# Local attention: the token shift ahead of the feed-forward made by three transfers within SBUF in place of TensorE products with shift matrices

## The chip, the cores and the metric

The kernel runs on one core of a Trainium2 chip. A core has five engines that run their own instruction lists and meet only at semaphores: TensorE (PE in the profile; PEld is its weight load), VectorE (DVE), ScalarE (ACT), GpSimd (POOL) and SyncE (SP), which here only issues transfers. The metric is the device time of one execution in microseconds (us), lower is better.

## The reference

A four-stage model over 8 sequences of 256 tokens of 128 features: dense attention, a routed feed-forward of 16 experts, a similarity counter, and last two layers of local attention with a gated feed-forward. Only the last stage is touched. Cut to what matters:

```python
def shift_token(t):
    t1, t2 = jnp.split(t, 2, axis=-1)                      # two halves of the features
    t2 = jnp.pad(t2, ((0, 0), (1, 0), (0, 0)))[:, :-1]     # second half: from the token before
    return jnp.concatenate([t1, t2], axis=-1)

def _layer(x, wqkv, qs, ksc, wo, lg, lb, w1, b1, w2, b2):
    h = shift_token(x)
    q, k, v = jnp.split(h @ wqkv, 3, axis=-1)              # to 8 heads of 64
    ...                                                    # l2norm, rotary, windows of 64 tokens
    x = x + o @ wo
    h = shift_token(x)                                     # the shift of this change
    h = (h - h.mean(-1, keepdims=True)) / jnp.sqrt(h.var(-1, keepdims=True) + 1e-05) * lg + lb
    a, g = jnp.split(h @ w1 + b1, 2, axis=-1)
    return x + (a * gelu(g)) @ w2 + b2
for l in range(2):
    x = _layer(x, ...)
```

## The kernel before

All arithmetic is f32 (the mask is bf16). The last stage works on 16 units, a unit being one layer of one sequence: 256 tokens as two tiles of 128 partitions (TB = 2), each with 128 features. Unit m is layer m // 8 of sequence m % 8. The stage is a software pipeline written out by hand: `run_steps` calls `step(n)` on each engine for n = -3 to 17, and the order of the calls inside an engine's `step` is the order of its instructions. In step n the attention of unit n runs beside the feed-forward of unit n - 1, the projections of units n + 1 and n + 2, and the end of unit n - 2. Nothing is scheduled by a planner; an engine that waits holds up all that stands behind it in its own list.

The names of one unit, with the lines of the kernel before:

- `scores1(n, a)`, PE: the mask (L1437) and the scores (L1450) of head pair a = 0 to 3. It waits for `f_e`, the exponentials of the pair before, since both use PSUM banks 0 and 1.
- `neg_max` on DVE (L1966, L1968) and `expo` on ACT (L1020, four exponentials each with its sum) follow every `scores1`.
- `attn_out(m)`, PE (L1484): the output projection; `residual_mid(m)`, DVE (L1989), adds the residual into SBUF tile `xm` and raises `f_xm`.
- `shift_mid(m)`, PE (L1492 to L1494): three f32 products of `xm` with the identity, with a shift matrix and with a carry matrix (for the first row of the second tile) leave the shifted tokens in the right half of PSUM bank 6 and raise `f_sh`.
- `stats_mid(m)`, DVE: `ln_stats` (L1566, L1569, L1571) on the shifted tokens; `ln_rstd`, POOL (L791): the power -1/2; `normed_mid(m)`, DVE: `ln_apply` (L1575).
- `turn_normed` (L1500), `hidden` (L1513) and `ffn_out` (L1523) on PE, `gelus` (L1047) on ACT, `gate` (L2013) on DVE: the feed-forward.
- `project1` (L1392), PE, and `rotate`, DVE (L1940 to L1949): queries and keys of unit n + 2, one quarter i after the other through one PSUM bank, with `square` on ACT (L994) between. `project_v` (L1406), PE: values of unit n + 1. `turn_probs1` (L1461) and DVE's `probs_out` (L1985): the turned probabilities.
- POOL: `add_rot` (L771), `normalise1` (L795), `copy_x` (L762), `inverse_norm` (L780, a power).

In SP's list the last stage has only the five stores of the result (L570): each waits for `h_out`.

Of the kernel before, what the change touches and what calls it, by code (L numbers as in the profile page):

```python
# [7 lines left out]
ALU = mybir.AluOpType  # L8
# [3 lines left out]
P = 128  # L12
# [43 lines left out]
def build_program(nc, A, out):  # L56

    with ExitStack() as ctx:
# [13 lines left out]
        identb = sb("identb", [P, P], BF16)  # L72
        causal = sb("causal", [P, P])
        band = sb("band", [P, TB, P], BF16)
        shift = sb("shift", [P, P])
        batch_rows = sb("batch_rows", [P, B])
        carry = sb("carry", [P, P])
        mhalf = sb("mhalf", [P, TB * H1])
        onecol = sb("onecol", [P, 1])
        lower = sb("lower", [P, P])  # L80
# [296 lines left out]
        rs1 = two(from_scratch, 2, TB)  # L377
        oT1 = two(from_scratch, PAIRS1, S)
        xm = two(from_scratch, TB, D)
        hn = from_scratch(TB, D)  # L380
        h2T = from_scratch(S)
        gl = from_scratch(3, S)
# [72 lines left out]
        def _(sp_):  # L455
# [109 lines left out]

            outc = out.rearrange("b (t p) d -> p (b t) d", p=P)
            for e, (o, n) in enumerate(ENDS):
                sp_.wait_ge(h_out, e + 1)
                sp_.dma_start(outc[:, o:o + n, :], x5[:, o:o + n, :]).then_inc(out_sem, 16)  # L570
            sp_.wait_ge(out_sem, 16 * len(ENDS))

        @block.gpsimd
        def _(pool):
            def row_rstd(c):
# [10 lines left out]
            pool.affine_select(out=causal[:], in_=causal[:], compare_op=ALU.is_ge, fill=0.0, base=0,  # L587
                               pattern=[[-1, P]], channel_multiplier=1)
            pool.memset(band[:], 0.0)
            pool.memset(shift[:], 0.0)  # L590
            pool.memset(carry[:], 0.0)
            pool.memset(batch_rows[:], 1.0)
            pool.memset(lower[:], 1.0)
            pool.memset(ones[:], 1.0)
# [4 lines left out]
                               pattern=[[0, TB], [-1, P]], channel_multiplier=1)  # L599
            pool.affine_select(out=batch_rows[:], in_=batch_rows[:], compare_op=ALU.is_ge, fill=0.0, base=0,  # L600
                               pattern=[[-H0, B]], channel_multiplier=1)
            pool.affine_select(out=shift[:], in_=shift[:], compare_op=ALU.not_equal, fill=1.0, base=1,
                               pattern=[[-1, P]], channel_multiplier=1)
            pool.drain()
            row_rstd(1)
            pool.affine_select(out=band[:], in_=band[:], compare_op=ALU.is_ge, fill=NEG, base=WIN,
                               pattern=[[0, TB], [1, P]], channel_multiplier=-1)
            pool.affine_select(out=batch_rows[:], in_=batch_rows[:], compare_op=ALU.is_ge, fill=0.0, base=H0 - 1,
                               pattern=[[H0, B]], channel_multiplier=-1)
            pool.affine_select(out=carry[:], in_=carry[:], compare_op=ALU.not_equal, fill=1.0,  # L610
                               base=-(P - 1), pattern=[[-1, P]], channel_multiplier=1)
            pool.drain()
            row_rstd(2)
            pool.memset(band[0:WIN, 1, WIN:P], 0.0)
# [464 lines left out]
        def _(pe):  # L1079
# [405 lines left out]
                                       start=(a == 0), stop=(a == PAIRS1 - 1))  # L1485
                mm.then_inc(f_wo, 1)

            def shift_mid(m, s):

                pe.wait_ge(f_xm, m + 1)  # L1490
                o = bank(6)[:, S:2 * S].rearrange("p (t d) -> p t d", t=TB)
                pe.matmul(o[:, :, 0:64], ident[:], xm[s][:, :, 0:64], start=True, stop=True, skip_group_check=True)  # L1492
                pe.matmul(o[:, :, 64:P], shift[:], xm[s][:, :, 64:P], start=True, stop=False, skip_group_check=True)
                pe.matmul(o[:, 1, 64:P], carry[:], xm[s][:, 0, 64:P], start=False, stop=True,  # L1494
                          skip_group_check=True).then_inc(f_sh, 1)

            def turn_normed(m):
                pe.wait_ge(f_hn, m + 1)
                for t in range(TB):
# [27 lines left out]
            def step(n, s):  # L1527
                if live(n + 2): project1(n + 2, s, 0)
                if live(n): scores1(n, s, 1)
                if live(n): turn_qk(n, s, 3)  # L1530
                if live(n - 1): attn_out(n - 1, 1 - s)
                if live(n): turn_probs1(n, 0)
                if live(n): scores1(n, s, 2)
                if live(n - 1): shift_mid(n - 1, 1 - s)
                if live(n + 1): project_v(n + 1, 1 - s, 0)
                if live(n + 1): project_v(n + 1, 1 - s, 1)
                if live(n): turn_probs1(n, 1)
                if live(n): values1(n, s, 0)
                if live(n): scores1(n, s, 3)
                if live(n + 2): project1(n + 2, s, 1)  # L1540
                if live(n + 1): turn_qk(n + 1, 1 - s, 0)
                if live(n - 1): turn_normed(n - 1)
                if live(n - 2): ffn_out(n - 2)
                if live(n + 3): turn_x(n + 3)
                if live(n): values1(n, s, 1)
                if live(n): turn_probs1(n, 2)
                if live(n + 2): project1(n + 2, s, 2)
                if live(n + 1): turn_qk(n + 1, 1 - s, 1)
                if live(n - 1): hidden(n - 1, 1)
                if live(n + 1): scores1(n + 1, 1 - s, 0)  # L1550
                if live(n): turn_probs1(n, 3)
                if live(n + 2): project1(n + 2, s, 3)
                if live(n): values1(n, s, 2)
                if live(n - 1): hidden(n - 1, 0)
                if live(n): values1(n, s, 3)
                if live(n + 1): turn_qk(n + 1, 1 - s, 2)
# [5 lines left out]
        def _(dve):  # L1562
# [364 lines left out]
                dve.memset(hT[s][64:P, 0:1], 0.0)  # L1927
            dve.memset(ssx[:], 1e-24)
            dve.memset(hg[64:P, 2, :], 1.0)
            dve.drain().then_inc(const_ready, 1)  # L1930
            dve.sem_inc(f_x, B)

# [62 lines left out]
                                  bank(7)[:, 0:S].rearrange("p (t d) -> p t d", t=TB), ALU.add).then_inc(f_x, 1)  # L1995

            def stats_mid(m):
                dve.wait_ge(f_sh, m + 1)
                ln_stats(lambda t: bank(6)[:, S + t * P:S + (t + 1) * P], TB, 0, f_var)

            def normed_mid(m):
                dve.wait_ge(f_rstd, m + 1)
                ln_apply(lambda t: hn[:, t, :], lambda t: bank(6)[:, S + t * P:S + (t + 1) * P],
                         TB, 0).then_inc(f_hn, 1)

            def gate(m):
                dve.wait_ge(f_a, m + 1)
# [108 lines left out]
```

## Time and profile before

| | |
|---|---|
| median of 3 runs | 933.12 us (931.44 to 933.57) |
| span of the profiled execution | 933.2 us |
| last stage, units 0 to 15 | from about 490 us to the end |
| busy over the span | PE 85%, DVE 71%, ACT 63%, POOL 57% |
| granted TensorE clock, mean | 0.927 of full speed |

The page gives the profiled execution's time as its span alone, 933.2 us, 0.1 us from the median. In the middle of the last stage one unit follows the other at a constant distance, so one unit can be read for all; the last four units run with less work beside them and are read one by one.

### The profile page before, as it was taken

The page shows a single profiled execution, that of the slowest core. Times are in us where ns is not written, and L with a number is a line of the kernel's source. Part 1 is how long each engine was busy: PE and PEld are TensorE (multiplying, and loading weights), DVE is VectorE, ACT ScalarE, POOL GpSimd, SP SyncE. Part 2 cuts the span into 40 slices and gives each one's busy share as a digit, 9 for nine tenths or more (in the row PEclk, how much of TensorE's full clock was granted, in tenths as well). Part 3 has the DMA queues.
Part 4 walks back from the last instruction along what each step waited for, and adds up shares of the span by engine and source line. Part 5 has one row for each costly group of instructions (what it writes and reads, how often), then busy time and mean ns, then how long its engine had stood idle before and what let it go on. Part 6 is the DMA issues. An engine that isn't in the chain of part 4 may idle for free. (4 is left out here: it accounts for less than half of the span.)

```text
span 933.2 us, 21526 instructions
## 1 busy us (share of the span) xinstructions
PE 789.5 (85%) x6366; PEld 587.0 (63%) x6366; DVE 663.4 (71%) x1986; ACT 588.5 (63%) x1784; POOL 527.3 (57%) x603
## 2 busy tenths in 40 slices
PE   5999999999989735982664789999999999998884
PEld 4777777777769735871551356666666666666664
DVE  5777777777776755553675577888888888887555
ACT  3688888888850103761441468888888888886660
POOL 4644444444442773326834867777777777775411
PEclk9999999999999856995785799999999999999998
DMA  8544444444400292431100000000000000000001
GB/s 223 186 156 152 152 152 152 152 152 152 152 27 1 61 311 64 113 96 46 43 12 0 1 1 2 1 2 2 1 2 1 1 2 2 1 2 2 12 2 34
DMA packets 61823, 61.28 MB, mean 66 GB/s; under 512 B 13244, under 2 KB 50607, under 8 KB 61615
## 3 DMA queue, kind: packets, MB, share of 16 engines
q1 hardware_dynamic: 59694, 56.10, 18.1%
q0 software_dynamic: 2048, 4.20, 1.6%
q8 instruction: 39, 0.64, 0.3%
q14 instruction: 42, 0.34, 0.1%
HBM read 17.55 MB, written 23.00 MB: 43 GB/s over the span
## 5 line engine op out<-in xcount | busy, mean ns | idle before, releaser
L643 POOL TENSOR_TENSOR scratch<-scratch 128x256 f32<-128x256 f32 (+1 forms) x128 | 105.7, 826 | 129.9 <-DVE scratch L1621 128.4
L1020 ACT ACTIVATE scratch<-psum,scratch 128x128 f32<-128x128 f32 x256 | 113.8, 458 | 49.2 <-DVE scratch L1968 47.4
L771 POOL TENSOR_TENSOR big<-big 128x512 f32<-128x512 f32 x64 | 81.2, 1269 | 70.1 <-DVE big L1949 70.1
L875 ACT ACTIVATE scratch<-psum,scratch 128x256 f32<-128x256 f32 x256 | 117.7, 478 | 2.9 <-DVE scratch L1639 2.8
L780 POOL TENSOR_TENSOR scratch<-scratch,mhalf 128x16 f32<-128x16 f32 x32 | 93.0, 2905 | 16.3 <-DVE scratch L1955 16.3
L1940 DVE TENSOR_REDUCE scratch<-big 128x8 f32<-128x512 f32 x64 | 43.7, 683 | 45.5 <-ACT big L994 45.3
L1125 PE MATMUL psum<-scratch 128*128 128x256 f32 x240 | 61.7, 380 | 0.0
L1632 DVE TENSOR_TENSOR psum<-psum,causal 128x512 f32<-128x512 f32 x64 | 44.8, 700 | 22.9 <-PE psum L1148 22.8
L1148 PE MATMUL psum<-scratch 64*128 64x128 f32 (+1 forms) x512 | 59.3, 350 | 0.0
L1169 PE MATMUL psum<-scratch 128*64 128x256 f32 (+1 forms) x512 | 55.7, 339 | 1.6 <-ACT scratch L884 1.6
L994 ACT ACTIVATE big<-psum 128x512 f32<-128x512 f32 x64 | 38.5, 602 | 29.0 <-PE psum L1392 28.9
L1158 PE MATMUL psum<-ident,scratch 128*128 128x128 f32 x384 | 56.0, 282 | 0.6 <-POOL scratch L643 0.5
L865 ACT ACTIVATE scratch<-psum,scratch 128x256 f32<-128x256 f32 x60 | 28.4, 474 | 42.9 <-PE psum L1125 42.9
L1966 DVE TENSOR_REDUCE scratch<-psum 128x4 f32<-128x512 f32 x64 | 44.0, 687 | 15.2 <-PE psum L1450 14.0
L875 ACT ACTIVATION_READ_ACCUMULATOR scratch<-psum,scratch 128x1 f32 x256 | 54.0, 211 | 0.0
L1020 ACT ACTIVATION_READ_ACCUMULATOR scratch<-psum,scratch 128x1 f32 x256 | 52.3, 204 | 0.0
L1169 PEld LDWEIGHTS psum<-scratch 128*64 128x64 f32 x512 | 31.1, 136 | 31.7 <-issue 20.2
L1472 PEld LDWEIGHTS psum<-scratch,big 128*64 128x64 f32 x768 | 34.5, 138 | 22.0 <-issue 21.5
L1158 PEld LDWEIGHTS psum<-ident,scratch 128*128 128x128 f32 x384 | 40.8, 140 | 11.9 <-issue 10.5
L795 POOL TENSOR_TENSOR scratch<-scratch 128x512 f32<-128x512 f32 x32 | 33.2, 1038 | 23.1 <-DVE scratch L1977 23.1
L1947 DVE TENSOR_TENSOR big<-psum,rot 128x512 f32<-128x512 f32 x64 | 43.5, 680 | 1.8 <-POOL big L771 1.8
L1437 PE MATMUL psum<-band,identb 128*128 128x256 bf16 x128 | 24.8, 276 | 23.2 <-ACT scratch L1020 21.7
(288 smaller groups left out, 2272.0 us busy)
## 6 DMA issues: line engine op xcount, KB each, us to landing
routed_in<-zfill SPq DMA_DIRECT2D x64, 256.0 KB, 2.1
scratch<-w_qkv SPq DMA_DIRECT2D x60, 193.0 KB, 2.2
scratch<-xT SPq DMA_DIRECT2D x60, 128.0 KB, 2.1
scratch<-routed_in SPq DMA_DIRECT2D x47, 64.0 KB, 1.9
routed_out<-scratch SPq DMA_DIRECT2D x23, 128.0 KB, 1.9
big<-in_L_ffn_W SPq DMA_DIRECT2D x1, 2048.0 KB, 8.7
stream<-in_L_attn_resid_pre SPq DMA_DIRECT2D x4, 256.0 KB, 3.6
big<-in_L_ffn_b SPq DMA_DIRECT2D x1, 1024.0 KB, 11.9
```

Source lines behind the costliest of these rows:

```text
L643: pool.tensor_tensor(y, y, rs[s][:, t, :].unsqueeze(2).to_broadcast([P, 2, n]), ALU.mult).then_inc(b_p, 1)
L771: pool.tensor_tensor(qk[s][t][:, j * INNER:(j + 1) * INNER], t1[i % 2], t2[i % 2], ALU.add).then_inc(f_add, 1)
L780: pool.tensor_tensor(o, ss[:, :, j * H1:(j + 1) * H1], half, ALU.pow).then_inc((f_rq, f_rk)[j], 1)
L875: last = act.activation(pr[s][:, t, h, :], scores_of(s)[:, h, t * S:(t + 1) * S], ACT.Exp, bias=nb[s][:, 2 * t + h:2 * t + h + 1], accum_o ...
L1020: last = act.activation(p1[k][:, h, t, :], bank(h)[:, t * P:(t + 1) * P], ACT.Exp, bias=nb1[k][:, h, t:t + 1], scale=rq8[s][:, t, 2 * a + ...
L1125: mm = pe.matmul(bank(6)[:, j * S:(j + 1) * S], w[:, j * P:(j + 1) * P], x, start=True, stop=True)
L1148: mm = pe.matmul(scores_of(s)[:, h, t * S:t * S + (t + 1) * P], qT[s][h * DH:(h + 1) * DH, t * P:(t + 1) * P], kT[s][h * DH:(h + 1) * DH, ...
L1158: mm = pe.transpose(turned_bank(h)[:, (kt + t) * P:(kt + t + 1) * P], pr[s][:, t, h, kt * P:(kt + 1) * P], ident[:])
L1169: mm = pe.matmul(bank(7)[h * 64:(h + 1) * 64, S + kt * P:2 * S], vS[r][:, kt, h * 64:(h + 1) * 64], pt[h][:, kt * S:kt * S + (TB - kt) * P ...
L1632: dve.tensor_tensor(diagonal, diagonal, mask, ALU.mult)
L1940: dve.tensor_reduce(ssx[:, t, j * H1:(j + 1) * H1, 0], o3(sq1[i % 2]), AX.X, ALU.add)
L1966: dve.tensor_reduce(mx1[k][:], psum[:, 0:2, 0:S].rearrange("p h (t n) -> p h t n", t=TB), AX.X, ALU.max)
```

## The change

`shift_mid` leaves PE's list and becomes three transfers in SP's list, from `xm` to a new SBUF tile `hs`: the second feature half one partition down, the row that crosses from the first tile to the second, and the first feature half unmoved. All three raise `f_sh`, and DVE's statistics wait for the three together. `ln_stats` and `ln_apply` read `hs` in place of PSUM bank 6. `hs` exists once; its one row without a token before it is set to zero once. The two matrices are no longer made on POOL. The five stores of the result stand between the transfers of the last units.

```diff
@@ -72,9 +72,7 @@
         identb = sb("identb", [P, P], BF16)
         causal = sb("causal", [P, P])
         band = sb("band", [P, TB, P], BF16)
-        shift = sb("shift", [P, P])
         batch_rows = sb("batch_rows", [P, B])
-        carry = sb("carry", [P, P])
         mhalf = sb("mhalf", [P, TB * H1])
         onecol = sb("onecol", [P, 1])
         lower = sb("lower", [P, P])
@@ -377,6 +375,7 @@
         rs1 = two(from_scratch, 2, TB)
         oT1 = two(from_scratch, PAIRS1, S)
         xm = two(from_scratch, TB, D)
+        hs = from_scratch(TB, D)
         hn = from_scratch(TB, D)
         h2T = from_scratch(S)
         gl = from_scratch(3, S)
@@ -565,9 +564,26 @@
 
 
             outc = out.rearrange("b (t p) d -> p (b t) d", p=P)
-            for e, (o, n) in enumerate(ENDS):
+
+            def shift_mid(m):
+
+                y = xm[m % 2]
+                sp_.wait_ge(f_xm, m + 1)
+                sp_.dma_start(hs[1:P, :, DH:D], y[0:P - 1, :, DH:D]).then_inc(f_sh, 16)
+                sp_.dma_start(hs[0:1, 1, DH:D], y[P - 1:P, 0, DH:D]).then_inc(f_sh, 16)
+                sp_.dma_start(hs[:, :, 0:DH], y[:, :, 0:DH]).then_inc(f_sh, 16)
+
+            def put_out(e):
+                o, n = ENDS[e]
                 sp_.wait_ge(h_out, e + 1)
                 sp_.dma_start(outc[:, o:o + n, :], x5[:, o:o + n, :]).then_inc(out_sem, 16)
+
+            for m in range(UNITS):
+                shift_mid(m)
+                if m in (UNITS - 4, UNITS - 2):
+                    put_out((m - UNITS + 4) // 2)
+            for e in range(2, len(ENDS)):
+                put_out(e)
             sp_.wait_ge(out_sem, 16 * len(ENDS))
 
 
@@ -587,8 +603,6 @@
             pool.affine_select(out=causal[:], in_=causal[:], compare_op=ALU.is_ge, fill=0.0, base=0,
                                pattern=[[-1, P]], channel_multiplier=1)
             pool.memset(band[:], 0.0)
-            pool.memset(shift[:], 0.0)
-            pool.memset(carry[:], 0.0)
             pool.memset(batch_rows[:], 1.0)
             pool.memset(lower[:], 1.0)
             pool.memset(ones[:], 1.0)
@@ -599,16 +613,12 @@
                                pattern=[[0, TB], [-1, P]], channel_multiplier=1)
             pool.affine_select(out=batch_rows[:], in_=batch_rows[:], compare_op=ALU.is_ge, fill=0.0, base=0,
                                pattern=[[-H0, B]], channel_multiplier=1)
-            pool.affine_select(out=shift[:], in_=shift[:], compare_op=ALU.not_equal, fill=1.0, base=1,
-                               pattern=[[-1, P]], channel_multiplier=1)
             pool.drain()
             row_rstd(1)
             pool.affine_select(out=band[:], in_=band[:], compare_op=ALU.is_ge, fill=NEG, base=WIN,
                                pattern=[[0, TB], [1, P]], channel_multiplier=-1)
             pool.affine_select(out=batch_rows[:], in_=batch_rows[:], compare_op=ALU.is_ge, fill=0.0, base=H0 - 1,
                                pattern=[[H0, B]], channel_multiplier=-1)
-            pool.affine_select(out=carry[:], in_=carry[:], compare_op=ALU.not_equal, fill=1.0,
-                               base=-(P - 1), pattern=[[-1, P]], channel_multiplier=1)
             pool.drain()
             row_rstd(2)
             pool.memset(band[0:WIN, 1, WIN:P], 0.0)
@@ -1485,15 +1495,6 @@
                                        start=(a == 0), stop=(a == PAIRS1 - 1))
                 mm.then_inc(f_wo, 1)
 
-            def shift_mid(m, s):
-
-                pe.wait_ge(f_xm, m + 1)
-                o = bank(6)[:, S:2 * S].rearrange("p (t d) -> p t d", t=TB)
-                pe.matmul(o[:, :, 0:64], ident[:], xm[s][:, :, 0:64], start=True, stop=True, skip_group_check=True)
-                pe.matmul(o[:, :, 64:P], shift[:], xm[s][:, :, 64:P], start=True, stop=False, skip_group_check=True)
-                pe.matmul(o[:, 1, 64:P], carry[:], xm[s][:, 0, 64:P], start=False, stop=True,
-                          skip_group_check=True).then_inc(f_sh, 1)
-
             def turn_normed(m):
                 pe.wait_ge(f_hn, m + 1)
                 for t in range(TB):
@@ -1531,7 +1532,6 @@
                 if live(n - 1): attn_out(n - 1, 1 - s)
                 if live(n): turn_probs1(n, 0)
                 if live(n): scores1(n, s, 2)
-                if live(n - 1): shift_mid(n - 1, 1 - s)
                 if live(n + 1): project_v(n + 1, 1 - s, 0)
                 if live(n + 1): project_v(n + 1, 1 - s, 1)
                 if live(n): turn_probs1(n, 1)
@@ -1927,6 +1927,7 @@
                 dve.memset(hT[s][64:P, 0:1], 0.0)
             dve.memset(ssx[:], 1e-24)
             dve.memset(hg[64:P, 2, :], 1.0)
+            dve.memset(hs[0:1, 0, DH:D], 0.0)
             dve.drain().then_inc(const_ready, 1)
             dve.sem_inc(f_x, B)
 
@@ -1995,13 +1996,12 @@
                                   bank(7)[:, 0:S].rearrange("p (t d) -> p t d", t=TB), ALU.add).then_inc(f_x, 1)
 
             def stats_mid(m):
-                dve.wait_ge(f_sh, m + 1)
-                ln_stats(lambda t: bank(6)[:, S + t * P:S + (t + 1) * P], TB, 0, f_var)
+                dve.wait_ge(f_sh, (m + 1) * 3 * 16)
+                ln_stats(lambda t: hs[:, t, :], TB, 0, f_var)
 
             def normed_mid(m):
                 dve.wait_ge(f_rstd, m + 1)
-                ln_apply(lambda t: hn[:, t, :], lambda t: bank(6)[:, S + t * P:S + (t + 1) * P],
-                         TB, 0).then_inc(f_hn, 1)
+                ln_apply(lambda t: hn[:, t, :], lambda t: hs[:, t, :], TB, 0).then_inc(f_hn, 1)
 
             def gate(m):
                 dve.wait_ge(f_a, m + 1)
```

On PE, in the step of a middle unit, this is the list before; `identb` with `band` is the mask at the head of `scores1`, `psum<-big` the scores, `wqkv` the projection of values:

```order
L1437 MATMUL psum<-band,identb 128x256 x2
L1450 MATMUL psum<-big 64x64 x2
L1450 MATMUL psum<-big 64x128 x6
L1492 MATMUL psum<-scratch,ident 128x2x64
L1493 MATMUL psum<-scratch,shift 128x2x64
L1494 MATMUL psum<-scratch,carry 128x64
L1406 MATMUL psum<-wqkv,scratch 128x512 x2
L1461 MATMUL psum<-ident,scratch 128x128 x4
```

And this is the same place in the changed kernel:

```order
L1447 MATMUL psum<-band,identb 128x256 x2
L1460 MATMUL psum<-big 64x64 x2
L1460 MATMUL psum<-big 64x128 x6
L1416 MATMUL psum<-wqkv,scratch 128x512 x2
L1471 MATMUL psum<-ident,scratch 128x128 x4
```

The three products are gone and nothing else moved on PE. On SP the last stage had only the stores; in the changed kernel the end of its list, from the transfers of unit 12 on, reads:

```order
L572 DMA scratch<-scratch 127x2x64
L573 DMA scratch<-scratch 1x16x4
L574 DMA scratch<-scratch 128x2x64
L579 DMA out<-stream 128x4x128
L572 DMA scratch<-scratch 127x2x64
L573 DMA scratch<-scratch 1x16x4
L574 DMA scratch<-scratch 128x2x64
L572 DMA scratch<-scratch 127x2x64
L573 DMA scratch<-scratch 1x16x4
L574 DMA scratch<-scratch 128x2x64
L579 DMA out<-stream 128x4x128
```

The first store moved between the transfers of units 12 and 13, the second behind those of unit 14; twelve more groups of three, for units 0 to 11, stand ahead, and the group of unit 15 and the other three stores follow.

## Rows read from the trace of the kernel before

**Rows 1.** Busy time by stretch, all engines; PEclk is the granted clock.
```profile
600.00:700.00 100.00, 94.08 (x894) 66.90 (x893) 81.12 (x201) 81.48 (x234) 72.29 (x59) 1.00 0.01 2
```
**Rows 2.** Chain of waits, middle unit: start us, us, what.
```profile
699.12 0.38 PE psum L1437 x2
...
700.10 0.42 PE psum L1492 x2
...
700.91 1.77 PE psum L1406 x4
...
703.72 0.33 PE psum L1437 x2
```
**Rows 3.** ACT by time, same unit: start us, us, line, operation.
```profile
698.77 0.21 ACT L1020 ACTIVATION_READ_ACCUMULATOR scratch<-psum,scratch 128x1 f32 x1
...
703.05 0.21 ACT L1020 ACTIVATION_READ_ACCUMULATOR scratch<-psum,scratch 128x1 f32 x1
...
706.70 0.46 ACT L1020 ACTIVATE scratch<-psum,scratch 128x128 f32<-128x128 f32 x1
```
**Rows 4.** SP by time, single issues from three stages.
```profile
3.39 0.23 SPq L462 DMA_DIRECT2D vrows<-in_L_attn_ln_b  x1
...
101.83 0.59 SPq L485 DMA_DIRECT2D scratch<-xT  x1
...
868.29 0.38 SPq L570 DMA_DIRECT2D out<-stream  x1
```
**Rows 5.** DMA issues of the page: count, KB each, us from issue to landing.
```profile
scratch<-xT SPq DMA_DIRECT2D x60, 128.0 KB, 2.1
scratch<-routed_in SPq DMA_DIRECT2D x47, 64.0 KB, 1.9
```
**Rows 6.** DVE by time, same middle unit.
```profile
698.85 0.41 DVE L1989 TENSOR_TENSOR scratch<-stream,psum 128x256 f32<-128x256 f32 x1
...
701.28 0.48 DVE L1566 BATCH_NORM_STATS2 st<-psum 128x6 f32<-128x128 f32 x2
...
703.76 0.72 DVE L1575 TENSOR_SCALAR scratch<-psum,mv,rstd 128x128 f32<-128x128 f32 x2
...
706.01 0.17 DVE L1968 TENSOR_TENSOR scratch<-scratch 128x4 f32<-128x4 f32 x1
```
**Rows 7.** POOL by time, same middle unit.
```profile
702.41 0.71 POOL L791 TENSOR_TENSOR rstd<-ve,mhalf 128x2 f32<-128x2 f32 x1 [1.08 <-DVE ve L1571]
703.08 0.40 POOL L762 COPY scratch<-stream 128x256 f32<-128x256 f32 x1
703.43 2.90 POOL L780 TENSOR_TENSOR scratch<-scratch,mhalf 128x16 f32<-128x16 f32 x1
```
**Rows 8.** Chain of waits, units 12 and 13.
```profile
845.25 0.44 PE psum L1492 x2
...
866.04 2.22 DVE stream L1575 x2
```
**Rows 9.** POOL by time, beside the last row.
```profile
866.91 1.26 POOL L771 TENSOR_TENSOR big<-big 128x512 f32<-128x512 f32 x1
```
**Rows 10.** DVE by time, units 14 and 15 and the end.
```profile
893.73 0.41 DVE L1989 TENSOR_TENSOR scratch<-stream,psum 128x256 f32<-128x256 f32 x1
...
898.34 0.50 DVE L1566 BATCH_NORM_STATS2 st<-psum 128x6 f32<-128x128 f32 x2 [0.53 <-PE psum L1494]
...
913.38 0.42 DVE L1989 TENSOR_TENSOR scratch<-stream,psum 128x256 f32<-128x256 f32 x1 [1.19 <-PE psum L1484]
914.78 0.49 DVE L1566 BATCH_NORM_STATS2 st<-psum 128x6 f32<-128x128 f32 x2 [0.97 <-PE psum L1494]
...
924.96 0.59 DVE L1575 TENSOR_SCALAR stream<-stream,mv,rstd 128x128 f32<-128x128 f32 x2
```
**Rows 11.** Busy time of PE alone by stretch, before unit 12's products.
```profile
842.00:844.00 2.00, 0.10 (x1) 1.00 0.00 0
846.00:848.00 2.00, 2.00 (x5) 0.50 0.04 8
```

## Prediction

> **What bounds the kernel now.** I read the stretches first, to see which engine is full where the shift stands. In the middle of the last stage PE is busy 94.08 of 100 us at full granted clock, while DVE, ACT and POOL have nearly a fifth of their time free or more [rows 1]. Work taken off PE there can therefore shorten the unit, if nothing else ends late. The chain of waits says what that would be. Of each unit it spends the stretch from 700.10 to 700.91, 0.81 us, on the three products of the shift, directly between the scores of head pair 2 and the projection of values [rows 2]. Upstream of them PE waits for the exponentials of pair 1: ACT ends at 698.77 + 0.21 = 698.98 and the mask of the next scores starts at 699.12, so a wake-up costs 0.14 [rows 2, 3]. This wait hides under nothing and stays. Last I read the instructions of the other engines by time, for the same unit: where ACT's exponentials end, when DVE has the residual and begins the statistics (701.28, right behind the shift), and what POOL does then [rows 3, 6, 7].
>
> **What goes: PE's products.** 0.81 us per unit leave PE, but PE cannot keep them all. Behind the shift stand the values, a turn, a product and then the scores of pair 3, at 703.72 [rows 2]. They would come at 703.72 - 0.81 = 702.91. They wait, however, for the exponentials of pair 2, whose last instruction ends at 703.05 + 0.21 = 703.26 [rows 3]; these start from scores that stand ahead of the shift, so the change does not make them earlier. With the wake-up of 0.14 PE starts at 703.40, and with 0.38 for a mask that starts from a wait against 0.33 for one in the stream it ends at 703.78 against 704.05 [rows 2]. The gain left is 0.27, rounded down to 0.26 us per unit: a new wait of about half a microsecond takes the rest. That holds for units 0 to 11, twelve of them, which follow the same pattern.
>
> **What comes: the transfers.** `residual_mid` ends at 698.85 + 0.41 = 699.26 [rows 6]. SP is idle and starts an issue 0.03 us after DVE's end: a store starts at 868.29 behind an instruction that ends at 866.04 + 2.22 = 868.26 [rows 4, 8]. The trace has no issue of this shape. A one-row issue takes 0.23, a 128-row one 0.38 (out of SBUF) to 0.59 (within SBUF) [rows 4]; I take 0.45 for the first, 0.23 for the single row, 0.05 between issues. The third then starts at 699.29 + 0.45 + 0.05 + 0.23 + 0.05 = 700.07. From issue to landing 64 KB into SBUF takes 1.9, 128 KB within SBUF 2.1 [rows 5]. The third carries 64 KB in runs of 256 bytes; I take 1.9, the row of its size. It lands at 701.97, and DVE starts its statistics at 702.0, 0.72 later than now. Bounds: 701.8 (issues of 0.38, a landing 0.1 quicker than any row of rows 5) to 702.5 (issues of 0.59, a landing of 2.2).
>
> The Trainium skill, page "DMA: Bandwidth & Descriptors", section "Anatomy of one DMA", puts one transfer, measured on GpSimd's path, at 2.0 us and the bytes at 436 GB/s. By it the third would take an estimated 2.15 and land 0.25 later than by the row, still inside these bounds.
>
> **What the later start moves.** From the statistics' start DVE and POOL need what they need now: POOL's power ends at 702.41 + 0.71 = 703.12, which is 1.84 behind 701.28 [rows 6, 7]. With 702.0 it ends at 703.84, and `normed_mid` starts at 703.87. Now it starts at 703.76 and takes 0.72 from PSUM [rows 6]; a pair with both sides in SBUF takes 0.59 [rows 10]. So it would end at 704.46 against 704.48: nothing lost. But as an instruction within SBUF it can be held by POOL. A pair of the same form at 866.04 took 2.22 and ended with POOL's two-input add, at 866.91 + 1.26 = 868.17 [rows 8, 9]. Behind the power POOL copies x, 703.08 + 0.40 = 703.48, which is 2.20 behind the statistics' start [rows 7]. If that copy holds `normed_mid`, it starts at 704.20 and ends at 704.79, 0.31 late.
>
> Queued behind it on DVE are a reciprocal, a product, and `neg_max` of pair 3, whose second half ends at 706.01 + 0.17 = 706.18 [rows 6]; ACT waits for that with the exponentials of pair 3, which start at 706.70 now [rows 3] and from which ACT runs without a gap to the exponentials that the next unit's scores need. If PE is to be 0.26 earlier, these must start at 706.44; with 0.03 from DVE to ACT the lateness allowed is 706.44 - 706.21 = 0.23. Beyond that each further 0.1 us late costs 0.1 of the gain. Unheld (-0.02) the gain stays 0.26; held (0.31) it is 0.18. I take 0.20 per unit: 12 x 0.20 = 2.4 us. At the bounds: 0.26 with a landing at 701.8; with 702.5 and the copy holding, the lateness is 0.81 and the gain 0.26 - 0.58 = -0.32, a loss.
>
> POOL waits for the statistics too, and its copy and `inverse_norm` (2.90) stand behind [rows 7]. They end 0.7 us later. POOL is the engine with the most time free, busy 72.29 of 100 us [rows 1], and I cost that at nothing; without this cover DVE's query scales and the rotated queries would come late by the same.
>
> **The last four units.** Here DVE waits more and PE idles more, so the transfer is mostly covered. Unit 12: the products are on the chain [rows 8], the exponentials are long done, DVE waits for PE: 0.8 gained. Unit 13 is alike: 0.8. Unit 14: the residual ends at 893.73 + 0.41 = 894.14, a landing 2.74 later (702.0 - 699.26) is at 896.9, and DVE's wait of 0.53 for the products goes [rows 10]: 0.5. Unit 15 has nothing beside it: the residual ends at 913.80, the statistics start at 914.78 now and at 913.80 + 2.74 = 916.54 then: 1.8 lost (1.6 to 2.3 at the bounds) [rows 10]. Together 0.8 + 0.8 + 0.5 - 1.8 = 0.3 gained.
>
> The stores cost nothing: the instructions that release the first stand ahead of unit 13's residual in DVE's list, and its issue takes 0.38 [rows 4], so SP is free again when the residual comes; the second stands in the same way ahead of unit 15's. The two matrices not made on POOL lie under the loading of the input, and the one-row memset is a fraction of a tenth.
>
> **Sum.** 933.2 - 2.4 - 0.3 = 930.5 us. The profiled execution is 0.1 above the median, so it stands as it is.
>
> **The rivals.**
>
> *Late landing* (slower). Place: DVE's `stats_mid` in the middle units; price: the gain falls one for one once `normed_mid` ends more than 0.23 late, and turns to a loss at 0.49. With the copy holding, that is a landing near 702.2, 2.9 us after the residual; without, near 702.5. At 702.5 and held: 12 x 0.32 = 3.8 lost, and the end gives 0.8 + 0.8 + 0.5 - 2.3 = -0.2: 933.2 + 4.0 = 937.2. For it: three issues in a row on one queue, each with its own price, and no row of this shape. Against: the rows put the landing at 702.0. Chance 0.18.
>
> *No change.* The same, half as bad: a gain of 0.05 per unit, 0.6, and nothing from the end: 932.6. Chance 0.27.
>
> *All of it.* If the exponentials of pair 2 were no limit, 12 x 0.81 = 9.7 and 0.3 would go: 923.2. Against it stands ACT's end at 703.26 [rows 3]; it would need ACT to run earlier than its scores allow. Chance 0.05.
>
> *POOL's power holds DVE.* If `normed_mid` loses not to the copy but to `inverse_norm` right behind it, 2.90 long, it is some 2.5 late, 2.5 - 0.23 - 0.26 = 2.0 lost per unit: 933.2 + 24 = 957. Against it: `neg_max` at 706.01, both inputs in SBUF, took 0.17 while that power ran from 703.43 to 706.33 [rows 6, 7]. Chance 0.02.
>
> The Trainium skill, "SBUF — State Buffer", section on who interferes with whom, says that a VectorE instruction in a two-port mode (a `tensor_scalar` within SBUF can enter it) and a GpSimd instruction fully block each other for the whole instruction. By that rule the copy holds `normed_mid`, and the power would too. The stall at 866.04 agrees with it; the unhindered 0.17 under the power does not support its last part.
>
> *The clock.* PE waits twice per unit instead of once. After a stretch with 0.10 of 2.00 us busy the granted clock was 0.50, that is 1.2 GHz [rows 11]; with 94% busy it was 1.00 [rows 1]. The new wait is short and 3 us from the other; at a cost of 1 us per unit it would be 933.2 + 12 = 945. Chance 0.01.
>
> That the change does not do what it says I see no room for: the products are gone from PE's list, and DVE waits for all three transfers.
>
> **How the numbers follow.** Forecast 0.47, no change 0.27, late landing 0.18, all of it 0.05, power or clock 0.03. A run of this kernel can tell 0.2%, 1.9 us, from no change. Faster: 0.47 + 0.05 = 0.52; same 0.27; slower 0.21. The forecast's own range is 928.7 to 931.5: at the low end 0.26 per unit, 3.1, and 1.4 from the end, if units 12 and 13 save 1.25 each, half-way to twice 0.8 at the half clock that follows their idle stretch [rows 11], and unit 15 loses 1.6; at the high end 0.12 per unit. The range to hold 8 in 10 reaches to the late landing and a little below the forecast: 926.5 to 937.
>
> **What would show it.** Right: PE loses 96 matmul records; the scores of pair 3 wait about 0.5 us for ACT; a transfer group lands 2.6 to 2.9 us after the residual; middle units shorter by about 0.2 us; the statistics of unit 15 about 1.8 us later behind their residual. Wrong: a landing beyond 3 us, `normed_mid` longer than 1 us, PE waiting at the projections of queries, a granted clock below 1.00 in the middle units, or middle units shorter by over 0.3.

## The result, and the profile after

The changed kernel takes 980.81 us, the median of 4 runs (976.15 to 985.37), against 933.1 before (931.44 to 933.57): a ratio of 1.0514, interval 1.0479 to 1.0549. The forecast was 930.5 in a range of 926.5 to 937, so it was wrong in sign and in size. The profiled execution spans 978.4 us, 45.2 more than before. A span is not a device time: where a run lists both, the time is 1.7 to 2.7 us longer (980.2 against 978.4 here), so the 933.2 that the prediction started from was an execution of some 935 us and not one 0.1 from the median. Its saving of 2.7 taken from the median gives 930.4, and nothing below hangs on it.

Busy time in the middle of the last stage of the changed kernel, columns as in [rows 1]:

```profile
600.00:700.00 100.00, 87.66 (x776) 61.06 (x774) 70.53 (x179) 71.66 (x211) 63.91 (x52) 0.94 0.03 7
```

Every engine does less in 100 us than before, and the granted TensorE clock is 0.94 where it was 1.00 [rows 1]. No engine became full; the list of waits shows what they wait for. Of units 0 to 13 of the changed kernel (who waits, for whom; us in total, times, longest):

```profile
DVE st L1566 <- DMA scratch<-scratch: 50.1, 13, 4.2
...
PE psum L1501 <- DVE scratch L1575: 24.6, 13, 2.4
```

DVE's statistics wait for the three transfers, and PE then waits for the rows that these statistics normalise. In a middle unit of the changed kernel, SP by time (L572 is the transfer of 127 rows, L573 the single row, L574 the half that is not shifted), and the summary of L573 over all units (ns, minimum/median/maximum):

```profile
715.55 0.70 SPq L572 DMA_DIRECT2D scratch<-scratch  x1
716.29 2.75 SPq L573 DMA_DIRECT2D scratch<-scratch  x1
719.09 0.66 SPq L574 DMA_DIRECT2D scratch<-scratch  x1
```
```profile
L573 SPq DMA_DIRECT2D scratch<-scratch x16: 2606/2737/2796, 555.1 to 954.6; - x16
```

DVE of the same unit, by time, against [rows 6]:

```profile
715.12 0.40 DVE L1990 TENSOR_TENSOR scratch<-stream,psum 128x256 f32<-128x256 f32 x1
...
721.38 0.49 DVE L1566 BATCH_NORM_STATS2 st<-scratch 128x6 f32<-128x128 f32 x2 [3.76 <-DMA scratch<-scratch]
...
723.25 0.65 DVE L1575 TENSOR_SCALAR scratch<-scratch,mv,rstd 128x128 f32<-128x128 f32 x2 [0.23 <-POOL rstd L801]
```

and POOL beside the last of these rows:

```profile
723.18 0.40 POOL L772 COPY scratch<-stream 128x256 f32<-128x256 f32 x1
723.53 2.90 POOL L790 TENSOR_TENSOR scratch<-scratch,mhalf 128x16 f32<-128x16 f32 x1
```

The residual ends at 715.52. SP starts 0.03 later, as forecast, but the third issue starts 3.57 behind the residual where the forecast had 0.81, and the statistics start at 721.38, 5.86 behind it; the forecast had 2.74. What the DMA engines did in these 7 us (40 slices of 0.175 us; tenths of the 16 engines' time, and GB/s):

```profile
DMA  0000000000000000000000000011001970000000
GB/s 0 0 0 0 0 0 0 0 0 0 1 12 18 18 18 19 18 19 18 18 19 13 19 18 19 18 18 20 18 19 25 215 163 9 0 0 0 0 0 0
```

For about 3.4 us the engines move 18 GB/s, at a busy share that mostly rounds to 0 tenths; one of sixteen engines would be 0.06. Then the 64 KB of the third transfer come at 215 GB/s, in two slices. The trace's packets agree: the first of them starts at 716.92 and the 254 pieces of 256 bytes follow each other every 14 ns, 3.6 us in all; 256 B in 14 ns is 18 GB/s.

What the late landing does to PE is read from two groups of rows. First the kernel before, behind the stretch of [rows 2] (the turn of the normalised rows L1500, the feed-forward L1523, values L1472, turns L1461, queries L1428):

```profile
705.97 0.38 PE L1500 MATMUL psum<-ident,scratch 128*128 128x128 f32 x2
706.19 1.50 PE L1523 MATMUL psum<-wf,scratch 128*128 128x128 f32 x12
...
707.84 0.67 PE L1472 MATMUL psum<-scratch,big 128*64 128x128 f32 x12
708.44 0.66 PE L1461 MATMUL psum<-ident,scratch 128*128 128x128 f32 x4
...
709.79 0.60 PE L1428 MATMUL psum<-ident,big 128*128 128x128 f32 x4
```

The same products in the changed kernel:

```profile
723.97 0.44 PE L1501 MATMUL psum<-ident,scratch 128*128 128x128 f32 x2 [1.90 <-DVE scratch L1575]
724.24 1.69 PE L1524 MATMUL psum<-wf,scratch 128*128 128x128 f32 x12
...
726.29 1.12 PE L1482 MATMUL psum<-scratch,big 128*64 128x128 f32 x12
727.35 1.12 PE L1471 MATMUL psum<-ident,scratch 128*128 128x128 f32 x4
...
729.40 0.60 PE L1438 MATMUL psum<-ident,big 128*128 128x128 f32 x4
```

and the stretches of the changed kernel around it (PE busy first, the granted clock in the third column from the end):

```profile
719.00:723.00 4.00, 2.80 (x34) 1.51 (x30) 1.47 (x6) 2.86 (x8) 0.49 (x1) 1.00 0.11 24
723.00:727.00 4.00, 3.04 (x26) 2.71 (x28) 3.62 (x10) 1.36 (x7) 3.43 (x3) 0.80 0.00 0
727.00:731.00 4.00, 4.00 (x24) 3.02 (x23) 1.79 (x8) 3.37 (x10) 3.27 (x4) 0.77 0.02 4
```

The loss of a unit can be read off these rows, each start counted from the unit's own residual. The turn starts at 723.97 - 715.12 = 8.85 where it stood at 705.97 - 698.85 = 7.12: 1.73 late, because PE waits 1.90 for DVE. From there to the products of L1438 PE takes 729.40 - 723.97 = 5.43 where it took 709.79 - 705.97 = 3.82: 1.61 more for the same products, behind PE's wait, at a granted clock that has fallen from 1.00 to a mean of 0.80 and 0.77. Its two levels are 1.2 and 2.4 GHz, so 40 to 46% of these 8 us, some 3.4, ran at the lower; twelve products of L1482 take 1.12 where they took 0.67. Together 3.34, and the unit is 27.26 against 23.91 from residual to residual: 3.35 longer. What each part would be without the other, these rows alone do not tell; no_row and row_first below do.

Over the span, by the starts of the residuals: from unit 0's to unit 11's 298.2 against 261.9, 36.3 more; from there to unit 15's 101.4 against 95.0, 6.5 more; from the last residual to the end 25.1 against 19.8, 5.3 more, its statistics 5.94 behind the residual. The first residual comes 2.8 earlier; that start lies between 553.5 and 556.7 in the executions of all kernels here with no order in it, and I explain nothing by it.

### The profile page after: what moved, and what is told of

Read it like the earlier page. It is cut to its first block and busy times, and to the rows that moved or that the text cites. A ratio compares the mean times of both kernels' runs of the same rounds, so it can differ in the third digit from the quotient of the medians.

```text
span 978.4 us, 21377 instructions
## 1 busy us (share of the span) xinstructions
PE 796.1 (81%) x6270; PEld 587.5 (60%) x6270; DVE 659.8 (67%) x1987; ACT 589.1 (60%) x1784; POOL 526.3 (54%) x599
## 5 line engine op out<-in xcount | busy, mean ns | idle before, releaser
L1632 DVE TENSOR_TENSOR psum<-psum,causal 128x512 f32<-128x512 f32 x64 | 44.8, 700 | 23.0 <-PE psum L1158 22.9
L801 POOL TENSOR_TENSOR rstd<-ve,mhalf 128x2 f32<-128x2 f32 x16 | 11.3, 705 | 88.1 <-DVE ve L1571 88.1
L1482 PEld LDWEIGHTS psum<-scratch,big 128*64 128x64 f32 x768 | 38.1, 150 | 23.5 <-issue 23.2
L1566 DVE BATCH_NORM_STATS2 st<-scratch 128x6 f32<-128x128 f32 x48 | 11.3, 284 | 60.4 <-DMA scratch<-scratch 59.9
L1482 PE MATMUL psum<-scratch,big 128*64 128x64 f32 (+1 forms) x768 | 47.4, 264 | 0.0
```

Source lines behind the costliest of these rows:

```text
L1482: mm = pe.matmul(bank(2 + a % 2)[h * DH:(h + 1) * DH, t * P + o:t * P + o + n], v[:, (2 * a + h) * DH:(2 * a + h + 1) * DH], pt1[a % 2][:, ...
```

## The experiments

The open question was which transfer costs the time. The profile puts 2.75 us beside the single row; the theory is that this is only where SP stands while the 127 rows of the issue before go out one behind the other on one engine. The rival is that the single row, a transfer from the last partition to the first, is itself slow. In each kernel the count that DVE waits for follows the number of transfers.

**rows126**: one row fewer in the first transfer, everything else as in the change.

```
-  sp_.dma_start(hs[1:P, :, DH:D],     y[0:P - 1, :, DH:D]).then_inc(f_sh, 16)
+  sp_.dma_start(hs[1:P - 1, :, DH:D], y[0:P - 2, :, DH:D]).then_inc(f_sh, 16)
```

> The first transfer carries 126 rows instead of 127; the last shifted row of both tiles is left out, everything else is as in the changed kernel. 
Measured: 930.66 us, ratio 0.9972 (0.9957 to 0.9986). SP, and DVE's statistics, in a middle unit:

```profile
694.73 0.87 SPq L572 DMA_DIRECT2D scratch<-scratch  x1
695.65 0.56 SPq L573 DMA_DIRECT2D scratch<-scratch  x1
696.25 0.67 SPq L574 DMA_DIRECT2D scratch<-scratch  x1
```
```profile
698.32 0.49 DVE L1566 BATCH_NORM_STATS2 st<-scratch 128x6 f32<-128x128 f32 x2 [1.51 <-DMA scratch<-scratch]
```

The single row now takes 0.56, and the statistics start 3.61 behind the residual's end (694.71). One row of 127 is worth 50 us of the kernel (980.81 - 930.66): the count of rows is the cause, and not their bytes. The landing, by which I mean from here on the distance from the residual's end to the statistics' start, is 2.25 sooner (3.61 for 5.86), but the unit is 4.17 shorter (23.09 for 27.26), so something else came back with it, which the next runs show. The landing is later than the 3.2 expected, and unit and time lie below their ranges all the same.

**no_row** leaves the single row out. **row_first** issues it ahead of the 127 rows.

```
 sp_.dma_start(hs[1:P, :, DH:D], y[0:P - 1, :, DH:D]).then_inc(f_sh, 16)
-sp_.dma_start(hs[0:1, 1, DH:D], y[P - 1:P, 0, DH:D]).then_inc(f_sh, 16)    # no_row: gone; row_first: one line up
 sp_.dma_start(hs[:, :, 0:DH], y[:, :, 0:DH]).then_inc(f_sh, 16)
```

> The single row that crosses from the first tile to the second is left out; 127 rows and the unmoved half remain. Theory A: the hold moves to the issue behind the 127 rows, so the unmoved half now issues for some 2.7 us and lands at most 0.7 us earlier: 965 to 981 us. Theory B: 2.79 us less in front of the last transfer, landing 3.0 us after the residual: 932 to 945 us.

> Same three transfers, the single row first. Theory A: its issue takes 0.3 to 0.8 us, and the 2.7 us move to the unmoved half, which now stands behind the 127 rows; time as the changed kernel, 970 to 985 us. Theory B: the single row's issue takes 2.7 us in its new place; time the same.

Measured: no_row 962.48 us, ratio 1.0305 (1.0281 to 1.0329); row_first 984.41 in a single execution. SP of no_row, then of row_first (there L572 is the single row, L573 the 127):

```profile
711.14 0.67 SPq L572 DMA_DIRECT2D scratch<-scratch  x1
711.86 2.65 SPq L573 DMA_DIRECT2D scratch<-scratch  x1
```
```profile
692.30 0.56 SPq L572 DMA_DIRECT2D scratch<-scratch  x1
692.90 0.70 SPq L573 DMA_DIRECT2D scratch<-scratch  x1
693.64 2.78 SPq L574 DMA_DIRECT2D scratch<-scratch  x1
```

The long issue is whichever stands behind the 127 rows, even the transfer that is quick elsewhere; the single row takes 0.56 when it stands ahead of them. The rival falls.

no_row came out below what the surviving theory expected, though its landing is hardly sooner: 5.70 in the unit shown, against 5.86. The difference is in what follows. Busy time of no_row, then DVE and PE of the same unit:

```profile
600.00:700.00 100.00, 90.66 (x830) 61.09 (x829) 71.57 (x192) 77.80 (x224) 69.33 (x56) 1.00 0.03 7
```
```profile
710.71 0.41 DVE L1989 TENSOR_TENSOR scratch<-stream,psum 128x256 f32<-128x256 f32 x1
...
716.82 0.48 DVE L1565 BATCH_NORM_STATS2 st<-scratch 128x6 f32<-128x128 f32 x2 [3.59 <-DMA scratch<-scratch]
...
733.95 0.17 DVE L1968 TENSOR_TENSOR scratch<-scratch 128x4 f32<-128x4 f32 x1
```
```profile
719.40 0.44 PE L1500 MATMUL psum<-ident,scratch 128*128 128x128 f32 x2 [1.73 <-DVE scratch L1574]
...
723.91 0.60 PE L1437 MATMUL psum<-ident,big 128*128 128x128 f32 x4
```

PE waits 1.73, nearly as long as in the changed kernel, but the granted clock stays at 1.00, and the unit takes 25.18 where the changed kernel's takes 27.26. Of the 2.08 between them 0.16 stand ahead of the turn of the normalised rows (8.69 for 8.85), 0.92 between the turn and the products of L1437 (4.51 for 5.43), and the rest, 1.0, behind these; there DVE's small product of 128x4 in `neg_max` takes 0.17 in no_row (733.95) and 1.26 in the changed kernel (739.33), which is the subject of before_wait below. row_first has both kinds of unit in one execution. Its units 5 and 6, columns as in [rows 1]:

```profile
691.90:717.60 25.70, 22.48 (x207) 15.27 (x208) 18.07 (x49) 19.29 (x56) 17.48 (x14) 1.00 0.03 7
717.70:745.30 27.60, 24.12 (x211) 16.72 (x208) 19.05 (x49) 19.86 (x58) 17.49 (x14) 0.94 0.02 5
```

Its units 1 to 10 all have a landing of 6.28 to 6.34. The three in which the clock stays at 1.00 take 25.8, the other seven 27.6 to 27.7. Against 23.91 the late landing at an unlowered clock thus costs 1.27 at 5.70 (no_row) and 1.9 at 6.3 (row_first); for the changed kernel's 5.86, between the two, I estimate 1.4. The other 1.9 of its 3.35 come with the fall of the clock and with the long product in `neg_max` that goes with it in every such unit. Why the clock falls in one unit and not in the next, behind waits of about the same length, is not shown.

**split112** cuts the 127 rows into 112 and 15, and so keeps the whole result with four transfers.

```
-  sp_.dma_start(hs[1:P, :, DH:D], y[0:P - 1, :, DH:D]).then_inc(f_sh, 16)
+  sp_.dma_start(hs[1:113, :, DH:D], y[0:112, :, DH:D]).then_inc(f_sh, 16)
+  sp_.dma_start(hs[113:P, :, DH:D], y[112:P - 1, :, DH:D]).then_inc(f_sh, 16)
```

> The 127 rows are sent as 112 and 15, so four transfers per unit, same result. Theory A: 112 and 15 rows spread over many engines, all issues 0.3 to 0.8, landing about 4 us after the residual, middle units of about 25 us, 940 to 960 us. Theory B: the single row still issues for 2.7 us and one more issue stands in line: 985 to 1000 us.

Measured: 948.65, ratio 1.0154 (1.0094 to 1.0214). SP, and the statistics' wait over units 0 to 13:

```profile
705.84 0.62 SPq L572 DMA_DIRECT2D scratch<-scratch  x1
706.51 0.92 SPq L573 DMA_DIRECT2D scratch<-scratch  x1
707.47 0.59 SPq L574 DMA_DIRECT2D scratch<-scratch  x1
708.10 0.69 SPq L575 DMA_DIRECT2D scratch<-scratch  x1
```
```profile
DVE st L1567 <- DMA scratch<-scratch: 37.0, 14, 3.9
```

No issue is held, and a third of the loss is left. The issues themselves now take 2.26 us of the queue before the last can start (708.10 - 705.84), where the forecast had 0.78. In the unit shown the statistics start 4.37 behind the residual and the unit takes 23.84, no longer than before; the loss sits in unit 0, in the units where they start 5.4 to 6.0 behind it (1, 4, 7, 10, 11, 13) and at the end. In exactly these six the trace has a packet of 16 KB of the queue that the profile calls instruction (q8) running while the last pieces move.

**rows122** asks whether the number of engines is what counts, or 127 alone. The first transfer has 122 rows; the last five shifted rows are left out.

```
-  sp_.dma_start(hs[1:P, :, DH:D], y[0:P - 1, :, DH:D]).then_inc(f_sh, 16)
+  sp_.dma_start(hs[1:123, :, DH:D], y[0:122, :, DH:D]).then_inc(f_sh, 16)
```

> The changed kernel with 122 rows in the first transfer, twice a prime; the last five shifted rows of both tiles are left out. If the largest divisor up to 16 of the row count is the number of engines, 122 rows run on two: 122 packets each at 14 ns, 1.7 us instead of 3.6; the next issue is held for about 1 us instead of 2.74, landing about 4 us after the residual, middle units of 24.5 to 25.5 us, 940 to 955 us. If only 127 is special: like 126 rows, 928 to 933 us.

Measured: 938.5 in a single execution. GB/s of the DMA engines in 7 us of a middle unit, rows122 and then rows126 (slices as above):

```profile
GB/s 0 0 0 0 0 0 0 0 0 26 38 35 35 38 36 38 35 35 124 226 66 0 0 0 0 0 0 0 0 0 0 0 0 0 0 0 0 0 0 0
```
```profile
GB/s 0 0 0 0 0 0 0 0 0 7 171 145 46 1 1 0 0 59 231 85 0 0 0 0 0 0 0 0 0 0 0 0 0 0 0 0 0 0 0 0
```

36 GB/s for 122 rows, twice the 18 of the 127; up to 171 for 126, all pieces of 256 bytes. So 127 is not special: 122 = 2 x 61 moves as on two engines, 126 = 9 x 14 as on many. The trace's packets of 4 bytes count the same way, as if each engine that takes part in a transfer ended with one: 33 in a middle unit of the changed kernel (1 + 16 + 16), 34 in rows122, 46 in rows126 (14 + 16 + 16), 17 in no_row. The landing is near the 4 expected (3.90), but most units take 23.4, below the 24.5 to 25.5, and the time, 938.5, lies below its range too. SP is held little: the single row's issue took 0.87 against 0.56, and the third its usual 0.66.

**dma_split** gives the landing that the prediction assumed: 112 and 15 rows on SP's queue, the single row issued by ACT, the unshifted half written by DVE as a second residual of half the width.

```
 sp_.dma_start(hs[1:113, :, DH:D], y[0:112, :, DH:D]).then_inc(f_sh, 16)
 sp_.dma_start(hs[113:P, :, DH:D], y[112:P - 1, :, DH:D]).then_inc(f_sh, 16)
...
 act.dma_start(hs[0:1, 1, DH:D], xm[m % 2][P - 1:P, 0, DH:D]).then_inc(f_sh, 16)     # on ACT, behind probs_out
...
 dve.tensor_tensor(hs[:, :, 0:DH], stream[:, bass.ds(m * TB, TB), 0:DH],
                   bank(6)[:, 0:S].rearrange("p (t d) -> p t d", t=TB)[:, :, 0:DH], ALU.add)
```

> Same result as the changed kernel. 127 rows as 112 and 15 on SP, the single row issued by ACT in the stretch where it idles, and the unmoved half written by DVE as a second, half as wide residual add instead of a transfer. Theory A: the last of three transfers in two queues is issued 0.7 us after the residual, not 1.5, all landed after 2.8 to 3.0 us, middle units of 22.7 to 23.1 us, 922 to 930 us. Theory B (three transfers cannot land sooner than the 3.6 us seen with 126 rows): 929 to 933 us.

Measured: 929.03, ratio 0.9956 (0.9938 to 0.9974). DVE by time:

```profile
692.07 1.28 DVE L1973 TENSOR_TENSOR scratch<-scratch 128x4 f32<-128x4 f32 x1
...
695.12 0.41 DVE L1994 TENSOR_TENSOR scratch<-stream,psum 128x256 f32<-128x256 f32 x1
...
698.24 0.49 DVE L1570 BATCH_NORM_STATS2 st<-scratch 128x6 f32<-128x128 f32 x2 [0.61 <-DMA scratch<-scratch]
```

The statistics start 2.71 behind the residual's end (695.53); 2.74 was assumed. Of units 1 to 10 five land so (2.71 to 2.74); they take 23.6 against 23.91, a gain of 0.3 where 0.20 was forecast. In the other five the statistics start 3.4 to 4.2 behind the residual, and yet these units take 22.9 to 23.7. From residual 11 to 15 (units 11 to 14) it gains 1.3 where 2.3 was forecast, and the end loses 1.7 (21.5 against 19.8) where 1.8 was. Where the landing is right, the terms of the sum come out near their forecast. The unit misses the 22.7 to 23.1 expected, and the time lies in the ranges of both theories.

What divides the two kinds of unit is the small product of DVE. Behind a landing of 2.74 or less the product in the next `neg_max` of pair 1 takes 0.9 to 1.3, beside an add of POOL; behind a later landing it takes 0.16 to 0.17, ahead of that add, which stands in POOL's list behind the work that waits for the statistics. In the 64 units from 1 to 10 of before, the changed kernel, rows126, no_row, row_first, split112, rows122 and dma_split in which the clock stays at 1.00 this holds without exception, and behind the later landings (3.37 to 6.34) a unit takes the landing plus 19.5. Later by 1 us is then longer by 1 us; but a landing of up to 4.4 is still no loss against the 23.91 of before, since the other order gives about 1 us back. The first row shown above, that product in 1.28, is the subject of the next run.

**before_wait** follows the other thing that the runs showed: in rows126 units shrank by 0.8 although the landing was 0.87 later than assumed. The products of the shift are left as they were; only POOL waits, ahead of an add, for the product of 128x4 that ends DVE's `neg_max` of pair 1.

```
 if live(n + 1): scale_keys(n + 1, 1 - s)
+if live(n): pool.wait_ge(f_nb, n * 4 + 2)
 if live(n + 1): add_rot(n + 1, 1 - s, 3)
```

> The kernel before, products on TensorE and all, with one wait added on POOL: the add of the rotated queries (add_rot(n + 1, 3), L771) starts only after neg_max of head pair 1. Theory A (port order: in the kernel before, neg_max's two-input instruction starts 0.03 us behind that add and stands 1.1 us behind it, 1.27 instead of 0.17; with 126 rows it slipped ahead of it, and that, not the products alone, gave 0.8 us per unit): neg_max takes 0.17, the exponentials and scores behind it come 0.9 us earlier, middle units of 22.9 to 23.2 us instead of 23.9, 918 to 927 us. Theory B (the unit got shorter with 126 rows only because PE had less to do): PE is the limit, the wait of 1.19 us moves elsewhere, 931 to 935 us.

Measured: 921.29, ratio 0.9861 (0.9831 to 0.9892), the unit 22.92. DVE's product of 128x4 and POOL's add of 128x512 beside it, by time: the kernel before (one line of each engine), then before_wait:

```profile
695.81 1.26 DVE L1968 TENSOR_TENSOR scratch<-scratch 128x4 f32<-128x4 f32 x1
```
```profile
695.78 1.27 POOL L771 TENSOR_TENSOR big<-big 128x512 f32<-128x512 f32 x1
```
```profile
691.67 0.16 DVE L1969 TENSOR_TENSOR scratch<-scratch 128x4 f32<-128x4 f32 x1
```
```profile
691.92 1.28 POOL L771 TENSOR_TENSOR big<-big 128x512 f32<-128x512 f32 x1 [0.22 <-DVE scratch L1969]
```

Before, POOL starts 0.03 us ahead, and DVE's 0.17 us become 1.26; ACT's exponentials and PE wait behind it. With the order set, DVE goes first and the unit is 1.0 shorter. In rows126 the same order came about by itself (0.16 at 715.44, POOL's add at 715.55), through its later landing, as in dma_split.

**dma_split_wait** is both of the last two.

> The last two together. If the wait of POOL and the lighter PE add up: middle units of 22.0 to 22.6 us, 910 to 920 us. If the port order had already turned by itself in the split version: within 2 us of it.

Measured: 918.21, ratio 0.9841 (0.9795 to 0.9888); most units 22.5 to 22.8, a little above the range expected. It beats both kernels. By the medians 11.8 of the 14.9 us gained are POOL's wait alone; the two intervals overlap, so what the transfers add to it is not told apart from nothing.

## Why the prediction was wrong

The step that failed is "The trace has no issue of this shape. A one-row issue takes 0.23, a 128-row one 0.38 (out of SBUF) to 0.59 (within SBUF) [rows 4]; I take 0.45 for the first, 0.23 for the single row, 0.05 between issues", with 1.9 from issue to landing [rows 5] and bounds of 701.8 to 702.5. In their place the first issue took 0.70, the single row's 2.75, held while the 127 rows ahead of it went out one behind the other at 18 GB/s, and from the third issue to the statistics it took 2.29. The prices for many rows were those of transfers of 128 rows, and 127 was taken to be like them. The statistics came 5.86 behind the residual instead of 2.54 to 3.24. The prices of the issues were too low without the hold as well: in rows126 they are 0.87 and 0.56, and the statistics start at 3.61, beyond the upper bound, which had 0.59 for the first issue and left the single row at 0.23. A bound from the rows was to be had only as a rate per engine, which no row of before gives for pieces of 256 bytes; so the range should have been far wider on the slow side.

The Trainium skill, page "DMA: Bandwidth & Descriptors", section "Why a DMA increments its semaphore by 16 and not by 1", has the rule that was not weighed: a transfer is spread over the largest number of engines up to 16 that divides the slowest dimension of both its sides, and it names 127 partitions as a case that gets one. The runs agree: 18 GB/s for 127 rows, 36 for 122, up to 171 for 126, where the divisors are 1, 2 and 14.

The other steps, one by one:

- *PE is freed of 0.81 us, and a short wait for ACT takes most of it.* Right in kind: the page counts 6270 PE records, 96 fewer, and the mask of pair 3's scores waits for ACT, about half as long as forecast (0.27 in the changed kernel, 0.17 in rows126, about half a microsecond forecast).
- *What is late next is `neg_max` of pair 3.* Not what bound it. With so late a landing PE itself waits 1.90 at the turn of the normalised rows, a wait the prediction did not list. By its own formula a landing of 5.86 would have cost 2.61 a unit; 3.35 was measured, and in no_row, where the clock stays up, 1.27 for a landing of 5.70, where the formula gives 2.45; most of that difference is the order of DVE and POOL, worth 1.0 in before_wait.
- *The clock, chance 0.01, "at a cost of 1 us per unit".* It was part of the loss. PE took 1.61 longer from the turn to L1438 at the lower granted clock; in no_row, at a clock of 1.00, the same stretch is 0.69 longer than before, a wait of PE for DVE of 0.36 included. With the order of DVE and POOL that goes with it the fall of the clock costs about 1.9 a unit, by row_first's two kinds of unit.
- *The copy of POOL holds `normed_mid`.* It did not: 0.65 at 723.25, with POOL's copy (723.18) and power (723.53) beside it. The price of 0.31 was for nothing. The page "SBUF — State Buffer", section "Who interferes with whom", of the Trainium skill would have it blocked if it were in a two-port mode; this trace shows no block, and cannot show the mode.
- *The late landing*, with a chance of 0.18, was the right mechanism at the wrong size: 937.2 for a landing of 3.24 behind the residual. It should have carried the shape of the transfer as its reason, not only "no row of this shape".
- *The last unit loses, the three before gain.* The loss was in the right place: 1.8 forecast, 5.3 with the real landing, 1.7 in dma_split with the assumed one. The gain of the units before it turned into a loss of 6.5 (units 11 to 14, from residual 11 to residual 15).
- *POOL's later work, costed "at nothing".* At the landing assumed this held: dma_split's units at 2.7 keep the order of before. With a landing of 3.37 or more POOL's add comes behind DVE's small product, and the unit gains about 1 us.
- *Missed altogether:* whether POOL's add or DVE's small product starts first, by hundredths of a microsecond, is worth 1 us a unit. The prediction said of PE's wait for the exponentials of pair 1 that it "hides under nothing and stays"; it is 1.19 in the kernel before and 0.18 in before_wait. rows126 comes to 930.66, beside the forecast of 930.5, for that reason and not for the forecast's, which is luck: with its landing of 3.61 the prediction's own formula gives a loss of 0.36 a unit, and it gained 0.8.

## What to carry to other kernels

Before a matrix product is replaced by a transfer, look at how many rows the transfer has and what divides that number: 127 rows cost 3.6 us of one engine and held the next issue on the queue for 2.7, 126 or 112 + 15 did not. A shape that no row of the trace shows is not bounded by its neighbours in size. Where a short instruction on DVE and a long add on POOL start within a tenth of a microsecond of each other, fix which goes first with a semaphore before trying anything larger: here that one line gave 11.8 us, where the whole change had been forecast to give 2.7.

## What the hardware showed that was not expected

An issue on SP can last long for a reason that is not its own: 2.6 to 2.8 us for any transfer behind the 127 rows, 0.56 to 0.69 for the same transfers elsewhere. In the rows shown the other issues within SBUF took 0.56 to 0.92, even for one row, against 0.23 for a row from memory [rows 4]; so splitting a transfer is not free. A wait of 1.90 us on PE was followed by a granted clock of 0.80 and 0.77 over the next 8 us, so that the unit lost nearly twice the wait; a wait of 1.73 in no_row was followed by none. Last, a landing can vary from unit to unit in one execution: in dma_split it is 2.7 to 3.0 in nine units and 3.4 to 4.2 in seven, and in exactly these seven a packet of 8 or 16 KB of the queues that the profile calls instruction (q8, q14) runs between issue and landing. No run takes these packets away, so the cause is not shown.
